# Resident up weights, moments on ScalarE and a later GpSimd job in the FFN stages of a one-core kernel

## Time and profile before

| what | us |
| --- | --- |
| median of 3 runs | 2672.25 (2670.08 to 2674.01) |
| the profiled execution | 2668.58 |
| its span, first to last instruction | 2666.9 |
| PE busy | 2489.1 (93%) |
| DVE busy | 1161.5 (44%) |
| ACT busy | 938.9 (35%) |
| POOL busy | 420.8 (16%) |

### The profile page before, as it was taken

How to read it: one execution, slowest core, us unless ns; L and a number is a source line. 1 busy time by engine, 2 the same in 40 slices (tenths; PEclk the granted TensorE clock), 3 DMA queues, 4 the chain that set the end, 5 groups by cost and what they waited for, 6 DMA issues and landing times. The chain is left out here.

```text
span 2666.9 us, 28817 instructions
## 1 busy us (share of the span) xinstructions
PE 2489.1 (93%) x11376; PEld 2049.3 (77%) x11376; DVE 1161.5 (44%) x1507; ACT 938.9 (35%) x1233; POOL 420.8 (16%) x296
## 2 busy tenths in 40 slices
PE   5887999999999999999899999999999999598984
PEld 4765788888878888888788888878888888477773
DVE  4875333322243334222433422233334222489995
ACT  3544434222233433222343322233333222255653
POOL 2783000000000000000000000000000000258886
PEclk9998999999999999999999999999999999799997
DMA  4544011021120112110211121120110111434342
GB/s 174 213 173 167 32 47 47 32 79 47 47 95 32 47 47 79 47 47 32 80 47 47 47 79 47 47 79 32 47 47 32 47 47 47 166 134 148 123 164 103
DMA packets 39194, 206.65 MB, mean 77 GB/s; under 512 B 4418, under 2 KB 4418, under 8 KB 18516
## 3 DMA queue, kind: packets, MB, share of 16 engines
q1 hardware_dynamic: 33364, 163.71, 17.3%
q0 software_dynamic: 5760, 41.95, 3.9%
HBM read 174.19 MB, written 31.46 MB: 77 GB/s over the span
## 5 line engine op out<-in xcount | busy, mean ns | idle before, releaser
L1113 DVE TENSOR_TENSOR h_lo<-g,h_hi 128x512 fp32r<-128x512 f32 x256 | 177.3, 693 | 756.3 <-ACT h_hi L1021 756.3
L57 PE MATMUL bank<-h_hi,w_hiB 128*128 128x512 f32 x1152 | 449.8, 390 | 11.7 <-DVE h_lo L1090 11.7
L59 PE MATMUL bank<-h_hi,w_loB 128*128 128x512 f32 x1152 | 448.9, 390 | 0.0
L58 PE MATMUL bank<-h_lo,w_hiB 128*128 128x512 f32 x1152 | 448.8, 390 | 0.0
L1018 ACT ACTIVATE g<-bank,bias_cols 128x512 f32<-128x512 f32 x256 | 176.4, 689 | 630.1 <-PE bank L59 393.3
L59 PE MATMUL bank<-o_hi,w_loA 128*128 128x512 f32 x768 | 299.2, 390 | 0.0
L58 PE MATMUL bank<-o_lo,w_hiA 128*128 128x512 f32 x768 | 299.1, 389 | 0.0
L57 PE MATMUL bank<-o_hi,w_hiA 128*128 128x512 f32 x768 | 299.1, 389 | 0.0
L960 ACT ACTIVATE w_hiB<-w_raw 128x2048 fp32r<-128x2048 f32 x37 | 71.0, 1919 | 565.6 <-PE bank L59 565.6
L1166 POOL COPY x_tok<-target_bias 128x1024 f32 x16 | 15.9, 1035 | 1591.2 <-PE bank L863 1591.2
L57 PEld LDWEIGHTS bank<-h_hi,w_hiB 128*128 128x128 f32 x1152 | 216.3, 188 | 58.2 <-issue 6.7
(11 more groups left out here) (210 smaller groups left out, 4402.3 us busy)
## 6 DMA issues: line engine op xcount, KB each, us to landing
w_raw<-in_units_a SPq DMA_DIRECT2D x32, 1024.0 KB, 4.8
w_raw<-in_units_b SPq DMA_DIRECT2D x32, 1024.0 KB, 4.8
w_raw<-in_w_packed SPq DMA_DIRECT2D x30, 1025.0 KB, 7.0
w_raw<-in_units_c SPq DMA_DIRECT2D x16, 1024.0 KB, 4.8
last_gain<-in_rows_packed SPq DMA_DIRECT2D x20, 512.0 KB, 4.3
x_tok<-x SPq DMA_DIRECT2D x16, 512.0 KB, 7.9
x<-stage SPq DMA_DIRECT2D x32, 256.0 KB, 2.3
first_gain<-in_rows_packed SPq DMA_DIRECT2D x10, 512.0 KB, 4.9
```

The costliest lines, as they stand in the source:

```text
L57: pe.matmul(out, lh, rh, start=(i == 0), stop=False)
L58: pe.matmul(out, lh, rl, start=False, stop=False)
L59: last = pe.matmul(out, ll, rh, start=False, stop=(i == len(terms) - 1))
L1113: v.tensor_tensor(h_lo[:, j, cols(n)], g[q % 2][:], h_hi[:, j, cols(n)].bitcast(F32), ALU.subtract).then_inc(hlo_done, 1)
```

## The change

1. **Up weights stay on chip.** All three (last stage: six) up matrices are loaded once, straight into `wu_lo`, and split once (`split_up(r)`, one per role and layer). PE and ACT pick the role's block by a register (`own_row`). The per-job load becomes the down half alone (`w_raw[:, 0:DOWN]`, 512 KB), and the down biases of all roles come in one DMA. In the last stage `gain` moves into the freed upper half of `w_raw`.
2. **Moments on ACT.** `var_eps` and `neg_mean` leave DVE's `aggregate` and become two ACT instructions, `moments(j - 2)`, at the start of ACT's pass j.
3. **Order on ACT.** In pass j: `moments(j - 2)`, both gelus, `norm(j - 2)` of two tiles, `transposed_hi(j + 1)`, `norm` of the other two, `split_down(j + 2)`. Before, pass j had `split_down(j + 1)` between gelu and `transposed_hi`.
4. **Order on DVE.** `split_down(j + 1)` comes first in pass j; `aggregate(j)` waits until ACT has read the moments of job j - 1.
5. **GpSimd one job later.** Pass j does `rstd_shift(j - 2)` and `gain_shift(j - 3)` with its scatter. The copies of row numbers are made once at the start. Two tiles of the last but one job and all of the last go to DVE.
6. **Order on PE.** As before, except that the register load stands before `transposes(j + 1)`, and that one half of the first fold comes after the last up.

SP's order is kept: `load_down(j + 2)`, then `load_gain(j)` with its wait for `add_done` of job j - 2.

```diff
 SP
-            def load_weights(j):
+            def load_down(j):
                 if j >= 2:
-                    sp.wait_ge(wdhi_done, 2 * (j - 2) + 2)
+                    sp.wait_ge(wdhi_done, j - 1)
                     sp.wait_ge(wdlo_done, j - 1)
-                    sp.wait_ge(wulo_done, j - 1)
-                sp.dma_start(w_raw[j % 2][:], ...
+                sp.dma_start(w_raw[j % 2][:, 0:DOWN], ...
+            def load_up(r):
+                sp.dma_start(wu_lo[:, r].bitcast(F32).rearrange("p k n -> p (k n)"),
+                             w_packed[layers[0] * ROLES + r, :, DOWN:DOWN + KB * D]).then_inc(wu_in[r // ROLES], 16)
             def load_gain(j):
                 if j >= 2:
                     sp.wait_ge(add_done, 2 * (j - 2) + 2)
...
-            load_weights(1)
+            for r in range(ROLES):
+                load_up(r)
+            load_down(1)
             ahead = (1, 2, 3, NJ - 2, NJ - 1)
             for j in range(NJ):
                 if j + 2 < NJ:
-                    load_weights(j + 2)
+                    load_down(j + 2)
                 load_gain(j)
...
+                if NL > 1 and j == 1:
+                    for r in range(ROLES, NB):
+                        load_up(r)
 ACT
+            def split_up(r):
+                act.wait_ge(wu_in[r // ROLES], 16 * ROLES)
...
+            def moments(j):
                 u = j % 2
                 if j >= 2:
+                    act.wait_ge(rstd_done, 2 * (j - 2) + 2)
+                act.wait_ge(aggr_done, GT * j + GT)
+                act.activation(var_eps[u], mean_var[:, :, 1], ACT.Identity, bias=eps).then_inc(moments_done, 1)
+                act.activation(neg_mean[u], mean_var[:, :, 0], ACT.Copy, scale=-1.0).then_inc(moments_done, 1)
...
+            for r in range(ROLES):
+                split_up(r)
+            split_down(1)
...
             for j in range(NJ):
-                split_up(j)
-                gelu(j)
+                row = own_row(act, j)
+                if j >= 2:
+                    moments(j - 2)
+                for m in range(KB):
+                    gelu(j, m, row)
+                if j >= 2:
+                    norm(j - 2, range(HALF))
                 if j + 1 < NJ:
-                    split_down(j + 1)
-                    transposed_hi(j + 1)
+                    for i in range(2):
+                        transposed_hi(j + 1, i)
                 if j >= 2:
-                    norm(j - 2)
+                    norm(j - 2, range(HALF, GT))
+                if j + 2 < NJ:
+                    split_down(j + 2)
+                if NL > 1 and 4 <= j < 4 + ROLES:
+                    split_up(ROLES + j - 4)
 DVE
             for j in range(NJ):
-                split_up(j)
-                hidden_lo(j, 0)
                 if j + 1 < NJ:
                     split_down(j + 1)
-                hidden_lo(j, 1)
+                for m in range(KB):
+                    hidden_lo(j, m)
...
 POOL
             for j in range(NJ):
                 if j + 2 < NG:
                     gather(j + 2)
                 if j >= 2:
                     rstd_shift(j - 2)
-                    gain_shift(j - 2)
-                    if j - 2 >= NJ - NG:
-                        scatter(j - 2)
+                if j >= 3:
+                    gain_shift(j - 3, range(2))
+                    if j - 3 >= NJ - NG:
+                        scatter(j - 3)
+            gain_shift(NJ - 3, range(2))
+            scatter(NJ - 3)
             rstd_shift(NJ - 2)
-            gain_shift(NJ - 2)
+            rstd_shift(NJ - 1)
+            gain_shift(NJ - 2, range(1, 2))
             scatter(NJ - 2)
-            rstd_shift(NJ - 1)
             scatter(NJ - 1)
```

More of the change, by code:

```diff
@@ L219, in ffn_layers @@
     HALF = GT // 2
+    DOWN = KD * BN
     with ExitStack() as ctx:
@@ L255, in ffn_layers @@
         dst_row = [sb(f"dst_row{g}", [P, 1], I32) for g in range(NG)]
-        bias_down = pair("bias_down", [P, KB])
+        bias_down = sb("bias_down", [P, NB, KB])
         stats = sb("stats", [P, GT, 6])
         mean_var = sb("mean_var", [P, GT, 2])
[L259 to L263, removed]
+        columns = sb("columns", [P, 10, GT])
+        var_eps, neg_mean, rstd, shift = ([columns[:, 2 * i + u, :] for u in range(2)] for i in range(4))
+        power = columns[:, 8, :]
+        eps = columns[:, 9, 0:1]
         turned = [ctx.enter_context(nc.psum_tensor(f"{tag}_turned{i}", [P, HALF, KD * P], F32)) for i in range(2)]
@@ L271, in ffn_layers @@
         gain_in = [sem(f"gain_in{u}") for u in range(2)]
+        wu_in = [sem(f"wu_in{n}") for n in range(NL)]
+        bias_in = sem("bias_in")
         rows_in = sem("rows_in")
@@ L407, in _ @@
                 down(j)
+                if j:
+                    row = own_row(pe, j - 1)
                 if j + 1 < NJ:
@@ L410, in _ @@
                 elif fold:
+                    pe.wait_ge(xlo_done, 2 * NJ)
                     fold_tiles(0, range(KD // 2))
                 if j:
[L413 to L416, removed]
+                    up(j - 1, range(GT), row)
+            up(NJ - 1, range(GT), own_row(pe, NJ - 1))
             if fold:
+                fold_tiles(0, range(KD // 2, KD))
                 fold_tiles(1, range(KD))
@@ new lines, in transposed_hi, with gelu @@
+            def transposed_hi(j, i):
+                act.wait_ge(tr_done, 2 * j + i + 1)
+                if j:
+                    act.wait_ge(down_done, KB * (j - 1) + KB)
+                cs = slice(i * HALF * P, (i + 1) * HALF * P)
+                act.activation(xT_hi[:, :, cs].rearrange("p k (i t) -> p i k t", i=HALF),
+                               turned[i][:].rearrange("p i (k t) -> p i k t", k=KD), ACT.Copy).then_inc(xhi_done, 1)
+            def gelu(j, m, row):
+                act.wait_ge(down_done, KB * j + m + 1)
+                act.activation(bank_D[m][:], bank_D[m][:], ACT.Gelu,
+                               bias=bias_down[:, bass.ds(row, 1), m:m + 1].rearrange("p a b -> p (a b)")).then_inc(gelu_done, 1)
+                if j >= 2 and m == 0:
+                    act.wait_ge(up_done, GT * (j - 2) + GT)
+                act.wait_ge(gelu_done, KB * j + m + 1)
+                act.activation(h_hi[j % 2][:, m, :], bank_D[m][:], ACT.Copy).then_inc(hhi_done, 1)
@@ L525, in aggregate, with gain_shift @@
                     v.bn_aggr(mean_var[:, t, :], stats[:, t, :]).then_inc(aggr_done, 1)
[L526 to L530, removed]
+            def gain_shift(j, tiles, before):
+                v.wait_ge(gain_in[j % 2], 16 * (j // 2 + 1))
+                for i, t in enumerate(tiles):
+                    v.wait_ge(norm_done, GT * j + t + 1)
+                    v.tensor_tensor(x[j % NX][:, t, :], x[j % NX][:, t, :], gain[j % 2][:, 0, :], ALU.mult).then_inc(last_mul, 1)
+                for i, t in enumerate(tiles):
+                    v.wait_ge(last_mul, before + i + 1)
+                    v.tensor_tensor(x[j % NX][:, t, :], x[j % NX][:, t, :], gain[j % 2][:, 1, :], ALU.add).then_inc(last_add, 1)
             split_down(0)
@@ L563, in _ @@
             aggregate(j)
[L564 to L569, removed]
-                    v.tensor_tensor(x[j % NX][:, t - 1, :], x[j % NX][:, t - 1, :], gain[j % 2][:, 1, :], ALU.add).then_inc(last_add, 1)
-            v.wait_ge(last_mul, GT)
-            v.tensor_tensor(x[j % NX][:, GT - 1, :], x[j % NX][:, GT - 1, :], gain[j % 2][:, 1, :], ALU.add).then_inc(last_add, 1)
+            gain_shift(j - 1, range(HALF), 0)
+            gain_shift(j, range(GT), HALF)
         @block.gpsimd
@@ L578, in rstd_shift, with gain_shift @@
                 pool.wait_ge(moments_done, 2 * j + 2)
-                pool.tensor_tensor(rstd[u][:], var_eps[u][:], power[:], ALU.pow).then_inc(rstd_done, 1)
+                if j >= 2:
+                    pool.wait_ge(norm_done, GT * (j - 2) + GT)
+                pool.tensor_tensor(rstd[u], var_eps[u], power, ALU.pow).then_inc(rstd_done, 1)
                 pool.wait_ge(rstd_done, 2 * j + 1)
-                pool.tensor_tensor(shift[u][:], neg_mean[u][:], rstd[u][:], ALU.mult).then_inc(rstd_done, 1)
-            def gain_shift(j):
+                pool.tensor_tensor(shift[u], neg_mean[u], rstd[u], ALU.mult).then_inc(rstd_done, 1)
+            def gain_shift(j, halves):
                 u = j % 2
                 pool.wait_ge(gain_in[u], 16 * (j // 2 + 1))
-                for i in range(2):
+                for i in halves:
                     ts = slice(i * HALF, (i + 1) * HALF)
@@ L620, in _ @@
             pool.memset(raw_rows[:], 0.0).then_inc(rows_zeroed, 1)
+            for j in range(2):
+                pool.tensor_copy(src_row[j][:], tab_src[:, j:j + 1]).then_inc(row_ready, 1)
+                gather(j)
             pool.memset(up_rows[:].bitcast(F32), 0.0).then_inc(rows_zeroed, 1)
[L622 to L625 removed]
+            pool.memset(power, -0.5).then_inc(const_ready, 1)
+            pool.memset(eps, LN_EPS).then_inc(const_ready, 1)
```

(5 more changed lines are left out.)

121 lines of the change are left out of this document (65 added, 56 removed).

## The result

The changed kernel takes 2770.22 us (median of four runs, 2767.95 to 2771.99) against 2671.48 of the kernel before, measured beside it: a ratio of 1.037 (1.035 to 1.039), 98.7 us slower. The profiled execution has a span of 2766.2, which is 99.3 more than before.

What follows compares the result with a forecast made beforehand. A loop through ACT, POOL and SP, closing once per job, was taken as the bound: 2.7 + 9.5 + 1.9 + 4.9 + 1.15 = 20.2 us. Over 20 turns, with starts and tails, 2672.25 + 84 = 2756 us, range 2716 to 2796.

Steps and rivals of the forecast that it cites:

- The circle: Per-job loop through ACT's moments, POOL's gain_shift, SP's wait and down load, ACT's split_down: 20.2 us, bounds 18.7 and 23.
- signs that were named: Profile signs: ACT's split waiting 5 to 9 us for w_raw, POOL idle 8, PE and DVE 65 to 70% busy.
- T to the first multiplication: From ACT beginning moments(j - 2) to POOL's first multiplication, behind DVE's wd_lo and the power: 2.7 us, 1.9 without collision.
- landing: Arrival of the 512 KB down weights behind gain: 4.9 us, between 4.2 and 6.7; 1.5 more with scatters in flight.
- The upper bound of 23: Upper bound, in us per job, on the circle's length, forecast at 20.2.
- T(3) = 79: First stage: ACT begins the moments of its pass 3 at 79 us, with zero net startup cost, bounds -3 and +5.
- One waits behind a 1 MB factor, 3: First stage: one of five turns, all with a scatter at 21.7 us, waits 3 us more behind a 1 MB factor.
- The shorter circle: Rival: faster landing and no collision, 18.7 us a turn and 2726 us, or 17.7 and 2706; chance 0.15.
- The faster case: Rival: PE's order sets about 15.0 us a job, 2650 us, only if the circle is under 15.0; chance 0.06.
- PE's clock: Rival: PE cools to 1.2 GHz, needs up to 28 us a job and becomes the bound, 2910 us; chance 0.04.
- No difference: Rival: savings and circle cancel, at 15.7 us per job; chance 0.03.
- gather behind its scatter: First stage: gather(6) to gather(9) directly behind the scatter they wait for on POOL; could cost 2 us in four turns.

Runs made afterwards that it cites:

- e1: Changed kernel with SP issuing each down load one place earlier, ahead of the load_gain and its wait: 2654.89 us, ratio to before 0.994.
- e2: Changed kernel with gain_shift and scatter back in the same pass as rstd_shift, SP's order as changed: 2642.80 us, ratio to before 0.989.
- e4: Changed kernel with the down split of job j + 1 back between gelu and transposed copies on ACT and DVE: 2710.51 us.
- e3: Changed kernel with SP issuing down(j + 3) before gain(j), both still behind the wait for POOL's last addition: 2706.29 us.
- e5: Kernel of e1 with var_eps and neg_mean back on DVE behind the four BN_AGGR: 2660.76 us, 5.9 more than e1.
- e10: e6 plus two up tiles before PE's transposes and an earlier late power; then first transposed copies ahead of up splits and second down split: 2600.54 us.
- e9: Changed kernel with DVE's wd_lo behind both hidden_lo instead of first in the pass: 2781.65 us, 11 more than the change.
- e8: Changed kernel with only PE's and DVE's order altered, two up tiles ahead of the transposes: 2765.95 us, 4 less than the change.
- e6: Kernel of e1 with gather(6) to gather(9) of the first stage between POOL's two multiplications and two additions: 2633.72 us.

## Why the prediction was right

**The circle** is what happens, step by step. Of the signs that were named these are there: ACT's split is released by the DMA of `w_raw` in all 15 turns of the last stage, POOL waits 8 us for ACT's moments, SP issues the down load 1.9 to 2.2 after the last addition. Two had the wrong size: ACT idles 10.7 to 13.8 us before its split in those turns and not 5 to 9, and of PE and DVE, both put at 65 to 70%, PE is at 75 to 80% and DVE at 54% of the windows above. e1, e2 and e4 open it from its three sides (queue, POOL's lag, place of the split) and each gives back 60 to 127 us; e3 shortens it by two known terms and the time follows.

**The terms**, forecast and measured in the quiet turn shown above: T to the first multiplication 2.7 and 2.5; POOL's four operations 9.5 and 9.3; end to issue 1.9 and 2.2; landing 4.9 and 4.2 (median 4.5); split 1.15 and 1.0. Sum 20.2 and 19.2. The upper bound of 23 has no term behind it; with the 6.7 given for the landing the same terms make 22.0, and 30 and 15 above 2756 make 2801, not 2796. `var_eps`, which the prediction names beside the rule on two SBUF inputs, has one input only; that it waited for POOL shows in e5 (0.17 us for 1.17), and the case of two inputs shows in wd_lo, below. With a scatter in flight the turn is 21.7 and 21.7, which is luck: the quiet part was put 1 us too long and the landing's surcharge 1 us too short:

```profile
w_raw<-in_w_packed SPq DMA_DIRECT2D x4, 512.0 KB, 7.0
...
out_rows<-last_x,last_dst_row POOLq DMA_INDIRECT x4, 7.6
```

The down weights land in 7.0 there, 2.5 more than in a quiet turn, and not 1.5. The Trainium skill, "DMA: Bandwidth & Descriptors", section "Anatomy of one DMA", has its 2.0 us plus bytes over 436 GB/s for one transfer that GpSimd issues; the 3.2 is an estimate from it for a load that SP issues. The nearest to its case here is e3, first in its queue, at 3.7.

**What was too small.** The forecast was 84, the result 98.7. (1) "T(3) = 79": the startup was said to cost zero net, with bounds -3 and +5, in both stages. In the first it cost 5.6; e10 takes 14 us out of the two starts. The three splits wait for all 1.5 MB of up weights (ACT idles 6.3 us for them in the first stage), and this landing I had called a cover. (2) "One waits behind a 1 MB factor, 3": two turns do, those behind the waits of job 2 and job 3, and they take 25.7 and 25.4. (3) The turns with a gather in the last stage were put at the plain 20.2 and are 21.4 to 22.7: the gather is issued right behind POOL's addition, beside the loads of the circle, and in three of them ACT has an up split of 1.04 more on the path. Against this stand six quiet turns, 19.1 to 19.5 except one of 20.6, most of them 1 us shorter than forecast.

**The rivals.** The shorter circle, at 18.7 or less, did not come: most quiet turns lie between it and the 20.2, since the landing was 4.5 and the collision at the power is there (1.78 for 1.02 in e9). The faster case needed the circle under 15 us, and its shortest turn was 19.1. Its size was right all the same: opened, the kernel is at 2654.9 (2650 had been worked out), by the same bound, PE's third up tile. PE's clock did fall, to 0.74 to 0.93 in windows from 2400 us on (1.00 in e1), but it had no price here: in e8 the turns did not follow PE's order, and PE was not on the circle. "No difference" did not come.

**gather behind its scatter** was left to the range with 2 us in four turns. In the closed circle it hides almost wholly: the two turns with such a gather and no factor take 22.9 and 21.9, the turn behind them, with a scatter alone, 21.8. Opened, it is the bound of the first stage (e6).

## What to carry to other kernels

When an engine's work is put a job later, look for what waits for its end, and for what stands behind that wait in the same queue; when a consumer is put a pass earlier at the same time, write down the circle and add up its length before counting what the engines save. A load that needs nothing from a wait should be issued ahead of it. Where every engine is idle a good part of the time and each waits for another, as here, look for such a circle; the busy shares did not show it, the turn of one job from start to start did.

## What the runs showed of the hardware

The price of second place in a queue: the 512 KB of down weights take 3.7 us first (e3) and 4.5 behind another 512 KB, 7.0 with a 1 MB scatter besides (the change). And wd_lo costs POOL about 0.75 us when it meets a short power and 1.0 when it meets a long multiplication, while DVE itself waits 0.5 more (e9). The Trainium skill, "SBUF — State Buffer", section "SBUF: two separate sides", says that a DVE operation with two SBUF inputs and a GpSimd operation that reads SBUF exclude each other for a whole instruction, and the trace agrees, 1.02 for the power alone and 1.78 beside wd_lo.
